# Spatial mamba: two blocks of states scanned by one instruction across two PSUM banks

## The chip, the cores and the metric

The kernel runs on one core of a Trainium2 chip. The metric is the time on the device in microseconds (us) of one execution of the whole program, which computes four layers one after the other. The change touches one stage of the last layer.

## The reference, cut to what matters

The input is 4 images of 64 channels and 128 x 128 pixels. Layer 0 is an attention with a gate in the frequency domain, layer 1 a Fourier mixer with experts, layer 2 a low-pass filter, layer 3 two mamba branches, spatial and spectral, and their merging. The spatial branch treats all 65,536 pixels as one sequence, with 128 inner channels and 16 states per channel:

```python
xz = x @ in_w.T; xi, z = split(xz, 2)
xc = silu(causal_conv4(xi) + conv_b)
dt, Bm, Cm = split(xc @ xproj_w.T, [4, 20])
dt = softplus(dt @ dt_w.T + dt_b)
A = -exp(A_log)
dA  = exp(dt[..., None] * A)                       # decay
dBx = dt[..., None] * Bm[:, :, None, :] * xc[..., None]
h = dA_t * h + dBx_t                               # for each t, in order: the scan
y = einsum('bds,bs->bd', h, C_t) + xc * D
out = (y * silu(z)) @ out_w.T
```

## The kernel before, in words

Each engine has its own instruction queue and runs in order; semaphores join them. The program is a row of stages, each ended by a barrier over all engines. The changed stage is `spatial_mamba`.

**Tiling.** A long run of equal tokens in each image row (60 of them) is folded into one column, the jump column, so that a row takes KEPT = 69 columns. A chunk is 7 rows, NA = 483 columns, and there are NC = 74 chunks. The 128 channels x 16 states are 2048 recurrences. They are laid out as NBL = 16 blocks of 128 partitions; block k holds 8 channels with 16 states each. Blocks are handled as NP = 8 pairs j = 0..7 (blocks 2j and 2j + 1). Per pair and chunk:

- TensorE, `spread_dt(j)` (L2366): two matmuls with one-hot weights copy the step sizes `du[.., 0, :]` of 8 channels onto 128 partitions, into PSUM `p_d`. In the trace one fp32 matmul is two instructions. It waits until pair j - 2 has been scanned, since there are four banks of `p_d`, one for each block modulo 4.
- ScalarE, `decay` (L2495): two exponentials, in place in `p_d`, one for each block.
- TensorE, `spread_u(j)` (L2379), the same for the inputs, into `p_u`; VectorE, `feed(j)` (L2565): `p_u` times B into `bx`, both blocks by one instruction. For pair OWN = 3 the spreading is done by a transfer (`spread_own`) and the product by GpSimd (`own_feed`, L2311).
- VectorE, `scan(j)` (L2582): one `tensor_tensor_scan` for each block, `hs = p_d * state + bx`. Its start value is the last column of the same block in `hs`, left there by the chunk before; in chunk 0 it is the constant 0.0 and 32 columns are left off.
- GpSimd, `weigh(j)` (L2302): both blocks of `hs` times C into `hc`.
- TensorE, `total(q)` (L2393), for every two pairs: the sum over states into `p_y`.

Around that, per chunk: the projections of x, z, dt, B and C through `p_x` (L2329, L2330, L2335, L2341, L2350, L2355), their reads on ScalarE (`read_x` L2447 and L2448, `read_z`, `softplus_in` and `softplus_out`, `copy_b` L2482, `copy_c`, the sigmoid's logarithm and exponential), `silu` and `step_sizes` on GpSimd, the skip term (L2386), `gate` on VectorE (L2590), `project_out` (L2399) and the store.

**Order.** Each engine's order within a chunk is written out by hand in a call of `stream`, as pairs (lag, part): in the turn of chunk i, a part works on chunk i - lag. The first 10 and the last turns are written out, the middle is a loop of four chunks per turn. VectorE's order is feed(1), scan(0), feed(2), scan(1), gate of the chunk before, scan(2), feed(4), scan(3), feed(5), scan(4), feed(6), scan(5), feed(7), scan(6), feed(0) of the next chunk, scan(7). In TensorE's order spread_dt(j) mostly stands right ahead of a spread_u, with one other product behind them.

**Semaphores of the change.** `scanned` counts blocks (16 a chunk), `decay_ready` blocks, `dt_spread` pairs, `bx_ready` the seven feeds, `weighted` pairs. `after(eng, sem, n)` is a wait that is left out where n is a constant of zero or less.

Of the kernel before, what the change touches and what calls it, by code (L numbers as in the profile page):

```python
# [2121 lines left out]
def spatial_mamba(nc, x2, w_in, w_conv, w_z, conv_b, w_xd, w_dt, dt_b, w_brep, w_crep, w_b, a_log, a_log2, skip_d, w_out, one_hot, fold, ident,  # L2122
# [11 lines left out]
    with Stage(nc, "spa") as st:  # L2134
# [35 lines left out]
        bx = st.sb("bx", [128, NBL, NA])  # L2170
        hs = st.sb("hs", [128, NBL, NA])
# [8 lines left out]
        p_d = [st.ps(f"p_d{i}", [128, 512]) for i in range(4)]  # L2180
# [10 lines left out]
        (dt_spread, u_spread, decay_ready, bx_ready, scanned, weighted, summed, y_ready, out_done, out_copied) = (  # L2191
            st.sem(n) for n in ("dt_spread", "u_spread", "decay_ready", "bx_ready", "scanned", "weighted", "summed", "y_ready",
# [15 lines left out]
        def kept(t):  # L2208
            return t.rearrange("p k (r w) -> p k r w", w=KEPT)[:, :, :, 0:KEPT - 1]

# [53 lines left out]
        def _(pool):  # L2264
# [27 lines left out]
            def weigh(j0, j1):  # L2292

                def run(c, s, r):
                    if j0 == 0:
                        pool.wait_ge(c_copied, c + 1)
                    for j in range(j0, j1):
                        pool.wait_ge(scanned, c * NBL + (2 * j + 2))

                        after(pool, summed, c * 4 + (j // 2 - 1))  # L2300
                        k = 2 * j
                        nc.gpsimd.tensor_tensor(hc[:, k % 8:k % 8 + 2, :], hs[:, k:k + 2, :],  # L2302
                                                cr2[:, s % 2, :].unsqueeze(1).broadcast_to([128, 2, NA]), ALU.mult).then_inc(weighted, 1)
                return run

            def own_feed(c, s, r):
                pool.wait_ge(b_copied, c + 1)
                pool.wait_ge(u_in, 32 * c + 32)

                after(pool, scanned, (c - 1) * NBL + (2 * OWN + 2))  # L2310
                nc.gpsimd.tensor_tensor(kept(bx[:, 2 * OWN:2 * OWN + 2, :]), b_kept(s), kept(uc[:, :, :]), ALU.mult).then_inc(bx_pool, 1)  # L2311
# [4 lines left out]
        def _(pe):  # L2316
# [4 lines left out]
            nc.tensor.matmul(p_d[1][:, 0:2], wd[:, :], c0[:, 0:2], start=True, stop=True).then_inc(setup_pe, 1)  # L2321
            nc.tensor.matmul(p_d[2][:, 0:ST], xrep[:, :], wb[:, :], start=True, stop=True).then_inc(setup_pe, 1)
# [34 lines left out]
            def spread_dt(j):  # L2357

                def run(c, s, r):
                    pe.wait_ge(dt_step, 2 * c + 2)  # L2360

                    after(pe, scanned, c * NBL + (2 * j - 2))
                    for e in range(2):
                        g = 2 * (j % 2) + e
                        v = slice(32 * g, 32 * g + 32)
                        mm = nc.tensor.matmul(p_d[(2 * j + e) % 4][:, 0:NA], hot[v, j // 2, :], du[v, s % 2, 0, :], start=True, stop=True)  # L2366
# [45 lines left out]
        def _(act):  # L2412
# [18 lines left out]
            nc.scalar.activation(c0[:, 4:5], p_d[1][:, 0:1], ACT.Relu, bias=db[:, 0:1])  # L2431
            link(nc.scalar.activation(c0[:, 5:6], p_d[1][:, 0:1], ACT.Abs, bias=db[:, 0:1]))
# [57 lines left out]
            def decay(j0, j1):  # L2490

                def run(c, s, r):
                    for k in range(2 * j0, 2 * j1):
                        act.wait_ge(dt_spread, c * NP + (k // 2 + 1))
                        nc.scalar.activation(p_d[k % 4][:, 0:NA], p_d[k % 4][:, 0:NA], ACT.Exp, scale=av2[:, k:k + 1]).then_inc(decay_ready, 1)  # L2495
                return run

            def copy_out(c, s, r):
# [4 lines left out]
                else:  # L2503
# [3 lines left out]
            stream(act, NC, UA, HEAD, 4, (2, decay(0, 1)), (1, softplus_in), (2, decay(1, 2)), (1, softplus_out), (2, decay(2, 3)), (0, read_x),  # L2507
                   (2, decay(3, 4)), (3, copy_out), (0, read_z), (2, decay(4, 5)), (0, sigmoid_ln), (2, decay(5, 6)), (1, copy_b),
# [3 lines left out]
        def _(dve):  # L2512
# [21 lines left out]
            link(nc.vector.tensor_scalar(b0[:, :], p_d[2][:, 0:ST], c0[:, 7:8], None, ALU.mult))  # L2534
# [17 lines left out]
            nc.vector.tensor_copy(bx[:, :, :].rearrange("p k (r w) -> p k r w", w=KEPT)[:, :, :, KEPT - 1],  # L2552
# [4 lines left out]
            def feed(j):  # L2557

                def run(c, s, r):
# [4 lines left out]
                    after(dve, scanned, (c - 1) * NBL + (2 * j + 2))  # L2564
                    nc.vector.tensor_tensor(kept(bx[:, 2 * j:2 * j + 2, :]), b_kept(s), kept(p_u[:, :, 0:NA]), ALU.mult).then_inc(bx_ready, 1)  # L2565
                return run

            def scan(j):

                def run(c, s, r):  # L2570
                    for k in (2 * j, 2 * j + 1):
                        dve.wait_ge(decay_ready, c * NBL + (k + 1))
                        if k % 2 == 0:
                            if j == OWN:
                                dve.wait_ge(bx_pool, c + 1)
                            else:
                                dve.wait_ge(bx_ready, c * ND + (FED.index(j) + 1))

                            after(dve, weighted, (c - 1) * NP + (j + 1))
                        start = isinstance(c, int) and c == 0  # L2580
                        v = slice(SHIFT if start else 0, NA)
                        nc.vector.tensor_tensor_scan(hs[:, k, v], p_d[k % 4][:, v], bx[:, k, v], 0.0 if start else hs[:, k, NA - 1:NA],  # L2582
                                                     ALU.mult, ALU.add).then_inc(scanned, 1)
# [821 lines left out]
```

## Time and profile before

| | us |
|---|---|
| median of 3 runs | 7533.4 |
| lowest and highest | 7525.0, 7562.55 |
| profiled execution, time | 7550.36 |
| its span in the trace | 7548.5 |
| VectorE / TensorE / ScalarE / GpSimd busy, whole span | 5590.7 / 6575.4 / 3977.8 / 3832.4 |

The profile is of one execution. A busy time is the union of an engine's instructions; a matmul's end is modelled, so a busy TensorE is not one at its peak. Consecutive instructions on VectorE overlap a little in the trace, so the time that one takes of its queue is the distance from its start to the next start, not its length. The granted clock is a share of TensorE's full 2.4 GHz; 0.5 is the lower level, 1.2 GHz.

### The profile page before, as it was taken

Reading aid. Unit: us, or ns where it says so; the run is one execution under the profiler, and the core shown is the slowest. Engines: PE = TensorE matmul, PEld = TensorE weight load, DVE = VectorE, ACT = ScalarE, POOL = GpSimd, SP = SyncE. Lnnn points to the kernel's source line nnn. Section 1 sums busy time; section 2 is a strip of 40 time slices with the busy share of each in tenths; the row PEclk is TensorE's granted clock in tenths of the full one; section 3 lists DMA queues with packets and bytes.
Section 4 is the critical chain, followed back from the end, with each engine's and each line's share of the span. In section 5 each row is a group of like instructions: output and inputs, shape, how many; then the busy total and the mean of one; then the engine's idle time right before and its main releaser. Section 6 shows DMA issues by size and latency. Waiting matters only on the chain. (4 is left out here: it accounts for less than half of the span.)

```text
span 7548.5 us, 120463 instructions
## 1 busy us (share of the span) xinstructions
PE 6575.4 (87%) x36560; PEld 3443.7 (46%) x36560; DVE 5590.7 (74%) x5630; ACT 3977.8 (53%) x6794; POOL 3832.4 (51%) x2716
## 2 busy tenths in 40 slices
PE   8968699999967379687999999999989999999970
PEld 7852233333345134574222222222257777777750
DVE  4653677777712278103999999999979999999974
ACT  4424466666612457103666666666655555555532
POOL 0100122222200300002888888888879999999960
PEclk9989799999978689757999999999989999999985
DMA  2243234334355523533222222222200000000016
GB/s 70 72 169 124 68 99 100 100 99 101 96 127 151 229 81 100 130 86 56 37 37 36 37 37 37 39 39 38 29 16 10 10 10 10 10 10 10 8 40 190
DMA packets 638233, 518.91 MB, mean 69 GB/s; under 512 B 249981, under 2 KB 569251, under 8 KB 629563
## 3 DMA queue, kind: packets, MB, share of 16 engines
q1 hardware_dynamic: 637947, 515.62, 27.9%
q8 instruction: 115, 1.88, 0.1%
q14 instruction: 171, 1.40, 0.1%
HBM read 304.91 MB, written 171.32 MB: 63 GB/s over the span
## 5 line engine op out<-in xcount | busy, mean ns | idle before, releaser
L2582 DVE TENSOR_TENSOR_SCAN spa_hs<-spa_p_d,spa_hs,spa_bx 128x483 f32<-128x483 f32 x1168 | 1370.3, 1223 | 21.1 <-ACT spa_p_d L2495 21.1
L2302 POOL TENSOR_TENSOR spa_hc<-spa_hs,spa_cr 128x966 f32<-128x966 f32 x592 | 1219.0, 2069 | 240.7 <-DVE spa_hs L2582 239.3
L2725 POOL TENSOR_TENSOR spe_hc<-spe_hs,spe_bcu 128x1024 f32<-128x1024 f32 x520 | 1219.7, 2362 | 64.5 <-DVE spe_hs L2937 63.5
L2937 DVE TENSOR_TENSOR_SCAN spe_hs<-spe_p_d,spe_bx 128x1024 f32<-128x1024 f32 x520 | 1161.4, 2275 | 35.0 <-ACT spe_p_d L2885 31.7
L2812 PEld LDWEIGHTS spe_p_y<-spe_idt,spe_hc 128*128 128x128 f32 x8320 | 965.1, 192 | 143.8 <-issue 143.8
L1065 DVE TENSOR_REDUCE attention_nm<-attention_p_s 128x2 f32<-128x640 f32 x1024 | 789.1, 812 | 260.2 <-PE attention_p_s L922 259.1
L2812 PE MATMUL spe_p_y<-spe_idt,spe_hc 128*128 128x128 f32 x8320 | 978.2, 276 | 0.0
L1023 ACT ACTIVATE attention_pr<-attention_p_t 128x512 f32<-128x512 f32 x1280 | 710.7, 599 | 420.3 <-PE attention_p_t L945 289.1
L2495 ACT ACTIVATE spa_p_d<-spa_p_d,spa_av 128x483 f32<-128x483 f32 x1184 | 703.9, 633 | 428.3 <-PE spa_p_d L2366 426.2
L2885 ACT ACTIVATE spe_p_d<-spe_p_d 128x896 f32<-128x896 f32 x520 | 445.5, 900 | 759.1 <-PE spe_p_d L2795 758.8
L2366 PE MATMUL spa_p_d<-spa_du,spa_hot 32*128 32x483 f32 x2368 | 657.0, 630 | 56.5 <-DVE spa_hs L2582 48.4
L2565 DVE TENSOR_TENSOR spa_bx<-spa_br,spa_p_u 128x952 f32<-128x952 f32 x518 | 589.8, 1139 | 54.0 <-PE spa_p_u L2379 42.4
L2379 PE MATMUL spa_p_u<-spa_du,spa_hot 32*128 32x483 f32 x2072 | 575.3, 631 | 11.5 <-DVE spa_bx L2565 11.4
L2924 DVE TENSOR_TENSOR spe_bx<-spe_bcu,spe_p_bc 128x1792 f32<-128x1792 f32 x260 | 525.6, 2022 | 50.1 <-ACT spe_bcu L2877 17.3
L922 PE MATMUL attention_p_s<-attention_ks,attention_qs 96*128 96x320 bf16 x2048 | 454.9, 304 | 54.4 <-DMA attention_qs<-scratch_qp 38.0
L1128 POOL TENSOR_TENSOR attention_on<-attention_os,attention_rc 128x512 f32<-128x512 f32 x128 | 162.5, 1269 | 645.4 <-DMA attention_rc<-scratch_den 410.3
L2366 PEld LDWEIGHTS spa_p_d<-spa_du,spa_hot 32*128 32x128 f32 x2368 | 185.1, 187 | 530.5 <-DVE spa_hs L2582 306.4
L962 PE MATMUL attention_p_o<-attention_pr,attention_vs 128*32 128x512 f32 x3072 | 410.3, 606 | 0.4 <-ACT attention_os L1037 0.4
L945 PE MATMUL attention_p_t<-attention_qs,attention_ks 99*128 99x512 bf16 x1024 | 396.1, 388 | 6.4 <-DMA attention_qs<-attention_mr 4.8
L1897 PE MATMUL experts_p_x<-experts_fs,experts_wx 128*128 128x512 f32 x768 | 332.6, 597 | 47.4 <-DVE experts_bx L1923 47.4
L2795 PE MATMUL spe_p_d<-spe_wa,spe_dt 32*128 32x512 f32 x2080 | 340.1, 640 | 3.4 <-DVE spe_hs L2937 3.3
L2393 PE MATMUL spa_p_y<-spa_hc,spa_fd 128*32 128x483 f32 x2368 | 308.8, 594 | 5.0 <-POOL spa_hc L2302 3.7
(425 smaller groups left out, 10630.8 us busy)
## 6 DMA issues: line engine op xcount, KB each, us to landing
attention_qs<-scratch_qp SPq DMA_DIRECT2D x768, 64.0 KB, 2.8
spa_uc<-spa_du SPq DMA_DIRECT2D x148, 241.5 KB
attention_rc<-scratch_den SPq DMA_DIRECT2D x128, 256.0 KB
scratch_qp<-patch_parts SPq DMA_DIRECT2D x64, 384.0 KB, 2.3
spa_xt<-scratch_x SPq DMA_DIRECT2D x148, 121.5 KB, 2.7
front_xs<-in_x_dram SPq DMA_DIRECT2D x64, 256.0 KB, 3.0
scratch_xf<-front_out SPq DMA_DIRECT2D x128, 128.0 KB, 2.5
patch_x<-scratch_xf SPq DMA_DIRECT2D x8, 2048.0 KB, 19.8
```

What stands on the lines that cost most here:

```text
L1023: nc.scalar.activation(pr[:, v, :], p_t[v % 2][:, :], ACT.Exp, scale=HD ** -0.5).then_inc(exp_done[v % 2], 1)
L1065: nc.vector.tensor_reduce(nm[:, c.u, t, 2 * s:2 * s + 2], p_s[s][:, :, 0:NK], AX.X, ALU.max, negate=True).then_inc(s_max[s], 1)
L2302: nc.gpsimd.tensor_tensor(hc[:, k % 8:k % 8 + 2, :], hs[:, k:k + 2, :], cr2[:, s % 2, :].unsqueeze(1).broadcast_to([128, 2, NA]), ALU.mult ...
L2366: mm = nc.tensor.matmul(p_d[(2 * j + e) % 4][:, 0:NA], hot[v, j // 2, :], du[v, s % 2, 0, :], start=True, stop=True)
L2379: mm = nc.tensor.matmul(p_u[:, e, 0:NA], hot[v, j // 2, :], du[v, s % 2, 1, :], start=True, stop=True)
L2495: nc.scalar.activation(p_d[k % 4][:, 0:NA], p_d[k % 4][:, 0:NA], ACT.Exp, scale=av2[:, k:k + 1]).then_inc(decay_ready, 1)
L2565: nc.vector.tensor_tensor(kept(bx[:, 2 * j:2 * j + 2, :]), b_kept(s), kept(p_u[:, :, 0:NA]), ALU.mult).then_inc(bx_ready, 1)
L2582: nc.vector.tensor_tensor_scan(hs[:, k, v], p_d[k % 4][:, v], bx[:, k, v], 0.0 if start else hs[:, k, NA - 1:NA], ALU.mult, ALU.add).then_ ...
L2725: nc.gpsimd.tensor_tensor(hc[:, k, :, d, :].rearrange("p s d t -> p d s t"), hs[:, k % 2, d, :, :], rows, ALU.mult)\
L2812: mm = nc.tensor.matmul(p_y[:, px], hc[:, k, n].rearrange("p d t -> p (d t)"), idt[:, :], start=False, stop=(k == NSUB - 1 and n == ST - 1))
L2924: nc.vector.tensor_tensor(bx[:, k % 2, d], steps(k, d), rows_for(p_bc[k % 2][:, 0:TD], d), ALU.mult).then_inc(bx_ready, 1)
L2937: nc.vector.tensor_tensor_scan(hs[:, k % 2, d].rearrange("p d s t -> p (d s t)"), p_d[h][:, :], bx[:, k % 2, d].rearrange("p d s t -> p (d ...
```

## The change

The two blocks of a pair are scanned by one instruction of 2 x 483 + 1 = 967 columns. `p_d` becomes two tensors of two banks each, one for each pair modulo 2. Block 2j lies in columns 28 to 510 of its two banks, block 2j + 1 in columns 512 to 994, and column 511 between them, the last of the first bank, is set to 0.0 once in the setup. `bx` and `hs` get a column more per block (stride 484). At the column between the blocks the scan computes 0 * state + bx, so that `bx[:, 2j, NA]` is the state with which block 2j + 1 starts. ScalarE puts it there: `carry(h)` copies the last states of four odd blocks of `hs`, 128 x 4, into the reset columns of `bx`, twice a chunk, for use in the next chunk. The first block's start value is still read from `hs`. Chunk 0 keeps its separate scans, without start values.

`scanned` now counts pairs (8 a chunk); all that waits for it still waits for the end of the same pair. The scan waits for the decays of both blocks of the pair before it starts (before, for each block's own), and for the new semaphore `carried`.

```diff
-        bx = st.sb("bx", [128, NBL, NA])
-        hs = st.sb("hs", [128, NBL, NA])
+        bx = st.sb("bx", [128, NBL, NA + 1])
+        hs = st.sb("hs", [128, NBL, NA + 1])
...
-        p_d = [st.ps(f"p_d{i}", [128, 512]) for i in range(4)]
+        p_d = [st.ps(f"p_d{i}", [128, 1024]) for i in range(2)]
...
+        def block_of(j, e):
+
+            o = 512 if e else 511 - NA
+            return p_d[j % 2][:, o:o + NA]
+
+        def joined(t, j):
+
+            return t[:, 2 * j:2 * j + 2, :].rearrange("p e n -> p (e n)")[:, 0:2 * NA + 1]
...
-                        pool.wait_ge(scanned, c * NBL + (2 * j + 2))
+                        pool.wait_ge(scanned, c * NP + (j + 1))
...
-                        nc.gpsimd.tensor_tensor(hc[:, k % 8:k % 8 + 2, :], hs[:, k:k + 2, :],
+                        nc.gpsimd.tensor_tensor(hc[:, k % 8:k % 8 + 2, :], hs[:, k:k + 2, 0:NA],
...
-                    after(pe, scanned, c * NBL + (2 * j - 2))
+                    after(pe, scanned, c * NP + (j - 1))
...
-                        nc.scalar.activation(p_d[k % 4][:, 0:NA], p_d[k % 4][:, 0:NA], ACT.Exp, scale=av2[:, k:k + 1]).then_inc(decay_ready, 1)
+                        nc.scalar.activation(block_of(k // 2, k % 2), block_of(k // 2, k % 2), ACT.Exp, scale=av2[:, k:k + 1]).then_inc(decay_ready, 1)
...
+            def carry(h):
+
+                def run(c, s, r):
+                    act.wait_ge(scanned, c * NP + 4 * (h + 1))
+                    k = 8 * h
+                    nc.scalar.activation(bx[:, k:k + 8:2, NA:NA + 1], hs[:, k + 1:k + 8:2, NA - 1:NA], ACT.Copy).then_inc(carried, 1)
+                return run
+
-            stream(act, NC, UA, HEAD, 4, (2, decay(0, 1)), (1, softplus_in), (2, decay(1, 2)), (1, softplus_out), (2, decay(2, 3)), (0, read_x),
-                   (2, decay(3, 4)), (3, copy_out), (0, read_z), (2, decay(4, 5)), (0, sigmoid_ln), (2, decay(5, 6)), (1, copy_b),
+            stream(act, NC, UA, HEAD, 4, (2, decay(0, 1)), (1, softplus_in), (2, decay(1, 2)), (3, carry(1)), (1, softplus_out), (2, decay(2, 3)), (0, read_x),
+                   (2, decay(3, 4)), (3, copy_out), (0, read_z), (2, decay(4, 5)), (0, sigmoid_ln), (2, decay(5, 6)), (2, carry(0)), (1, copy_b),
...
+            for i in range(2):
+                link(nc.vector.memset(p_d[i][:, 511:512], 0.0))
...
-                    for k in (2 * j, 2 * j + 1):
-                        dve.wait_ge(decay_ready, c * NBL + (k + 1))
...
+                    dve.wait_ge(decay_ready, c * NBL + (k + 2))
...
+                    if isinstance(c, int) and c == 0:
+                        for e in range(2):
+                            last = nc.vector.tensor_tensor_scan(hs[:, k + e, SHIFT:NA], block_of(j, e)[:, SHIFT:NA], bx[:, k + e, SHIFT:NA],
+                                                                0.0, ALU.mult, ALU.add)
+                    else:
+
+                        dve.wait_ge(carried, 2 * c + (j // 4 - 1))
+                        last = nc.vector.tensor_tensor_scan(joined(hs, j), p_d[j % 2][:, 511 - NA:512 + NA], joined(bx, j), hs[:, k, NA - 1:NA],
+                                                            ALU.mult, ALU.add)
+                    last.then_inc(scanned, 1)
```

## Rows read from the trace of the kernel before

**Rows 1.** The page's groups: line, engine, op, names, shapes, count | busy us, mean ns | idle before.
```profile
L2582 DVE TENSOR_TENSOR_SCAN spa_hs<-spa_p_d,spa_hs,spa_bx 128x483 f32<-128x483 f32 x1168 | 1370.3, 1223 | 21.1 <-ACT spa_p_d L2495 21.1
L2302 POOL TENSOR_TENSOR spa_hc<-spa_hs,spa_cr 128x966 f32<-128x966 f32 x592 | 1219.0, 2069 | 240.7 <-DVE spa_hs L2582 239.3
...
L2937 DVE TENSOR_TENSOR_SCAN spe_hs<-spe_p_d,spe_bx 128x1024 f32<-128x1024 f32 x520 | 1161.4, 2275 | 35.0 <-ACT spe_p_d L2885 31.7
```

**Rows 2.** Busy time by stretch, with instruction counts; then granted clock, DMA share, GB/s.
```profile
core 0: us, PE busy (x) PEld busy (x) DVE busy (x) ACT busy (x) POOL busy (x), PEclk, DMA share, GB/s
3560.00:5480.00 1920.00, 1852.18 (x7839) 551.69 (x7840) 1877.63 (x1745) 1256.20 (x2093) 1671.26 (x943) 0.97 0.25 36
3850.00:3900.00 50.00, 49.07 (x190) 13.91 (x188) 44.09 (x42) 30.22 (x50) 38.24 (x24) 0.86 0.25 36
```

**Rows 3.** Waits in the stage, 3560 to 5480 us: total us, times, longest.
```profile
ACT spa_p_d L2495 <- PE spa_p_d L2366: 416.2, 373, 4.6
PEld spa_p_d L2366 <- DVE spa_hs L2582: 306.4, 343, 1.4
POOL spa_hc L2302 <- DVE spa_hs L2582: 236.0, 241, 4.0
```

**Rows 4.** VectorE's timeline over a chunk: start us, length us, instructions merged.
```profile
5047.73 2.34 DVE L2582 TENSOR_TENSOR_SCAN spa_hs<-spa_p_d,spa_hs,spa_bx 128x483 f32<-128x483 f32 x2
...
5053.26 0.65 DVE L2590 TENSOR_TENSOR spa_y<-spa_p_y,spa_xz 128x483 f32<-128x483 f32 x1
...
5056.05 1.14 DVE L2565 TENSOR_TENSOR spa_bx<-spa_br,spa_p_u 128x952 f32<-128x952 f32 x1
5057.09 2.35 DVE L2582 TENSOR_TENSOR_SCAN spa_hs<-spa_p_d,spa_hs,spa_bx 128x483 f32<-128x483 f32 x2
5059.34 1.14 DVE L2565 TENSOR_TENSOR spa_bx<-spa_br,spa_p_u 128x952 f32<-128x952 f32 x1
...
5070.23 2.35 DVE L2582 TENSOR_TENSOR_SCAN spa_hs<-spa_p_d,spa_hs,spa_bx 128x483 f32<-128x483 f32 x2
...
5079.05 0.66 DVE L2590 TENSOR_TENSOR spa_y<-spa_p_y,spa_xz 128x483 f32<-128x483 f32 x1
```

**Rows 5.** VectorE's timeline in chunk 0.
```profile
3545.80 2.08 DVE L2582 TENSOR_TENSOR_SCAN spa_hs<-spa_p_d,spa_bx 128x451 f32<-128x451 f32 x2
3547.79 1.12 DVE L2565 TENSOR_TENSOR spa_bx<-spa_br,spa_p_u 128x952 f32<-128x952 f32 x1
```

**Rows 6.** VectorE's timeline in the spectral stage.
```profile
6013.91 4.46 DVE L2937 TENSOR_TENSOR_SCAN spe_hs<-spe_p_d,spe_bx 128x1024 f32<-128x1024 f32 x2
```

**Rows 7.** Timeline of all engines in the same chunk as rows 4.
```profile
5053.99 1.08 PE L2366 MATMUL spa_p_d<-spa_du,spa_hot 32*128 32x483 f32 x4
5055.29 1.19 ACT L2495 ACTIVATE spa_p_d<-spa_p_d,spa_av 128x483 f32<-128x483 f32 x2
5056.96 0.68 PE L2366 MATMUL spa_p_d<-spa_du,spa_hot 32*128 32x483 f32 x2
...
5058.25 1.08 PE L2386 MATMUL spa_p_y<-spa_xz,spa_dg 128*128 128x483 f32 x2
...
5067.19 1.19 ACT L2495 ACTIVATE spa_p_d<-spa_p_d,spa_av 128x483 f32<-128x483 f32 x2 [0.67 <-PE spa_p_d L2366]
```

**Rows 8.** Instructions on the states and their inputs: duration ns min/median/max, first and last start.
```profile
L2582 DVE TENSOR_TENSOR_SCAN spa_hs<-spa_p_d,spa_hs,spa_bx x1168: 1190/1222/1303, 3561.0 to 5486.3; 128x483 f32<-128x483 f32 x195
L2311 POOL TENSOR_TENSOR spa_bx<-spa_br,spa_uc x74: 2034/2126/2232, 3538.1 to 5464.8; 128x952 f32<-128x952 f32 x74
```

**Rows 9.** ScalarE's small operations in the setup.
```profile
3490.67 0.20 ACT L2433 ACTIVATE spa_c<-spa_c 128x1 f32<-128x1 f32 x1
...
3491.46 0.31 ACT L2436 ACTIVATE spa_a<-spa_av,spa_c 128x16 f32<-128x16 f32 x1 [0.36 <-DVE spa_c L2530]
```

**Rows 10.** VectorE's last step of the setup.
```profile
3502.49 0.27 DVE L2552 COPY spa_bx<-spa_jump 128x112 f32<-128x112 f32 x1 [4.45 <-DMA spa_jump<-scratch_steady]
```

**Rows 11.** TensorE's timeline in a stretch of low clock.
```profile
3848.59 1.98 PE L2366 MATMUL spa_p_d<-spa_du,spa_hot 32*128 32x483 f32 x4
```

More of the change, by code:

```diff
@@ L2308, in own_feed @@
                 pool.wait_ge(u_in, 32 * c + 32)
[L2310 to L2311 removed]
+                after(pool, scanned, (c - 1) * NP + (OWN + 1))
+                nc.gpsimd.tensor_tensor(kept(bx[:, 2 * OWN:2 * OWN + 2, 0:NA]), b_kept(s), kept(uc[:, :, :]), ALU.mult).then_inc(bx_pool, 1)
             stream(pool, NC, UA, HEAD, 2, (2, own_feed), (2, weigh(0, 1)), (1, step_sizes), (2, weigh(1, 6)), (0, silu), (2, weigh(6, 8)))
@@ L2320, in _ @@
             pe.wait_ge(step, 4)
-            nc.tensor.matmul(p_d[1][:, 0:2], wd[:, :], c0[:, 0:2], start=True, stop=True).then_inc(setup_pe, 1)
-            nc.tensor.matmul(p_d[2][:, 0:ST], xrep[:, :], wb[:, :], start=True, stop=True).then_inc(setup_pe, 1)
+            nc.tensor.matmul(p_d[0][:, 512:514], wd[:, :], c0[:, 0:2], start=True, stop=True).then_inc(setup_pe, 1)
+            nc.tensor.matmul(p_d[1][:, 0:ST], xrep[:, :], wb[:, :], start=True, stop=True).then_inc(setup_pe, 1)
             pe.wait_ge(w_ready, 1)
@@ L2365, in run @@
                         v = slice(32 * g, 32 * g + 32)
-                        mm = nc.tensor.matmul(p_d[(2 * j + e) % 4][:, 0:NA], hot[v, j // 2, :], du[v, s % 2, 0, :], start=True, stop=True)
+                        mm = nc.tensor.matmul(block_of(j, e), hot[v, j // 2, :], du[v, s % 2, 0, :], start=True, stop=True)
                     mm.then_inc(dt_spread, 1)
@@ L2562, in run @@
                     dve.wait_ge(u_spread, c * ND + (FED.index(j) + 1))
-                    after(dve, scanned, (c - 1) * NBL + (2 * j + 2))
-                    nc.vector.tensor_tensor(kept(bx[:, 2 * j:2 * j + 2, :]), b_kept(s), kept(p_u[:, :, 0:NA]), ALU.mult).then_inc(bx_ready, 1)
+                    after(dve, scanned, (c - 1) * NP + (j + 1))
+                    nc.vector.tensor_tensor(kept(bx[:, 2 * j:2 * j + 2, 0:NA]), b_kept(s), kept(p_u[:, :, 0:NA]), ALU.mult).then_inc(bx_ready, 1)
                 return run
@@ L2570, in run @@
                 def run(c, s, r):
-                    for k in (2 * j, 2 * j + 1):
-                        dve.wait_ge(decay_ready, c * NBL + (k + 1))
[L2573 to L2583, printed above, removed]
+                    k = 2 * j
+                    dve.wait_ge(decay_ready, c * NBL + (k + 2))
+                    if j == OWN:
+                        dve.wait_ge(bx_pool, c + 1)
+                    else:
+                        dve.wait_ge(bx_ready, c * ND + (FED.index(j) + 1))
+                    after(dve, weighted, (c - 1) * NP + (j + 1))
+                    if isinstance(c, int) and c == 0:
+                        for e in range(2):
+                            last = nc.vector.tensor_tensor_scan(hs[:, k + e, SHIFT:NA], block_of(j, e)[:, SHIFT:NA], bx[:, k + e, SHIFT:NA],
+                                                                0.0, ALU.mult, ALU.add)
+                    else:
+                        dve.wait_ge(carried, 2 * c + (j // 4 - 1))
+                        last = nc.vector.tensor_tensor_scan(joined(hs, j), p_d[j % 2][:, 511 - NA:512 + NA], joined(bx, j), hs[:, k, NA - 1:NA],
+                                                            ALU.mult, ALU.add)
+                    last.then_inc(scanned, 1)
                 return run
```

12 lines of the change are left out of this document (6 added, 6 removed).

## The prediction

> **What bounds the kernel now.** The first view to read is the page's list of groups, for the place of the changed instruction [rows 1]: the scan at L2582 is the costliest group of the kernel, 1168 instructions of 1.223 us, all in the spatial mamba, and the engine sat idle only 21.1 us before them. The second is the table by stretches [rows 2]: over 1920 us of this stage VectorE is busy 97.8%, TensorE 96.5%, GpSimd 87%, ScalarE 65%. Two engines seem full, so the third view is what each waited for [rows 3]. TensorE waits for the scans 343 times before a spreading alone, so it follows VectorE; GpSimd waits for them too, 236 us; VectorE is idle only 1920 - 1877.6 = 42 us, half of it (21.1) for decays [rows 1]. The fourth is VectorE's own timeline [rows 4]: one chunk runs from the gate at 5053.26 to the gate at 5079.05, 25.79 us, with no idle time at all. It is made of seven feeds and eight pairs of scans and one gate. From start to start a feed takes 5057.09 - 5056.05 = 1.04, a pair of scans 5059.34 - 5057.09 = 2.25, and what is left for the gate is 25.79 - 7 x 1.04 - 8 x 2.25 = 0.51. VectorE sets the pace, and what leaves its queue leaves the span: 73 such chunks (1168 / 16) give 1883 us and the idle time 42, together 1925, and the trace has the scans of chunks 1 to 73 from 3561.0 to 5486.3 + 1.2, 1926.5 us [rows 8].
>
> **What the joined scan costs.** No row shows a scan of 967 columns, so its price comes from two neighbours. In chunk 0, where the start value is a constant, a pair of 451 columns takes 3547.79 - 3545.80 = 1.99, so one is 0.995 [rows 5]. In the spectral mamba a scan of 1024 columns, read straight across two PSUM banks, starts 4.46 - 2.27 = 2.19 us before the next one [rows 1, 6]. Between them each column costs (2.19 - 0.995) / 573 = 2.085 ns, and a start costs 0.995 - 451 x 0.002085 = 0.055. By the same line 483 columns with a constant would take 1.062; the real one, whose start value is read from hs, takes 2.25 / 2 = 1.125, so reading it costs 0.063 and the whole start 0.118. The joined scan has one start and one column more: 967 x 0.002085 + 0.118 = 2.134. Against 2.25 that saves 0.116 us a pair. The upper bound of what a start can be is this same 0.118, so a pair can't save more; the lower bound of the start that goes is 0.055, if the value from hs should turn out to be paid for elsewhere; and nothing at all is the far end. I take 0.116, since the rows on either side of 967 columns give it, and the one of 1024 has the bank boundary in it. Over 8 x 73 = 584 pairs: 68 us. Chunk 0 keeps its 16 separate scans.
>
> The Trainium skill, "Vector Engine (DVE) Microarchitecture Reference", section 5.2, gives a cost of about 75 ns per instruction after overlap, whatever the program. By that rule a pair would save 0.075 less one column, 0.073, and the change 43 us instead of 68; it lies between the 0.055 and the 0.118 of the rows here.
>
> **The wait for the second decay.** Block 2j's scan used to wait for its own decay alone; now it waits for both. The place to look is where a decay is nearest to its scan. In the chunk shown, TensorE starts the spreading for pair 3 at 5053.99, ScalarE's two decays run 5055.29 to 5056.48, and the pair's scans start at 5057.09 [rows 4, 7]: 0.61 spare with both decays done. The timeline has more to spare at the other pairs (at pair 7 decays end 5068.38, scans start 5070.23: 1.85). So the new wait costs nothing as things stand. But VectorE comes earlier now. The chain to that decay starts at the end of pair 0's scan (5050.07: spreading 2, the projection of x, two reads of x on ScalarE, the decays) and takes 6.41 us, none of them VectorE's pairs; on VectorE there lie 7.02 us, with two pairs of scans in them. 7.02 - 2 x 0.116 - 6.41 = 0.38, or some 0.3 after the semaphore. The cover holds; were it gone, each tenth of a microsecond would cost 7 us over 73 chunks, and what would be late next is pair 3's release of the spreading for pair 5.
>
> **TensorE.** It is idle 1920 - 1852 = 68 us, 0.93 a chunk [rows 2], and VectorE's speed-up takes 0.93, so by the busy share alone it would be full. But it has something to give back: where a spreading for the decays and one for a feed need not wait for each other, they run together, all eight matmuls from 5056.96 to the next product at 5058.25 in 1.29 us, while one spreading alone takes 1.08 [rows 7]; wherever TensorE is late, more of them meet. From spreading 2, released by pair 0's scan, to spreading 7, released by pair 5's, VectorE gets faster by 5 x 0.116 = 0.6 us, so TensorE comes at most 0.6 late there, where 1.85 is spare. No release point moves: each is the end of the same pair.
>
> **GpSimd.** It waits 236 us for scans, 3.2 a chunk [rows 3]; the new chunk takes away 8 x 0.116 = 0.93 and leaves 2.3. Reading hs in rows of 484 with a gap of one column is priced by its other product of nearly the same size, whose output has gaps too: median 2.13, at most 2.23, against a mean of 2.07 [rows 1, 8]. That is at most 0.16 x 8 = 1.3 us a chunk, still under what is left.
>
> **The carries.** ScalarE gets two copies of 128x4 per chunk, 148 in all. Nearest rows: 0.20 for one column, 0.31 for sixteen [rows 9]; I take 0.25. Both stand behind decays whose own spreadings already waited for the scans that the carries wait for, so the wait is over when they come. Queued behind the one are the softplus and decay 2, behind the other the copy of B (for which TensorE's next product waits) and decay 6; ScalarE idles 416 us, 5.7 a chunk, for the spreadings before its decays [rows 3], and these idle times take the copies in. The scans ask for the carry half a chunk later or more. Cost nothing; without that cover, 2 x 0.25 x 73 = 36 us at worst. The two memsets of the reset column lie ahead of a 4.45 us wait for a transfer in the setup [rows 10], which covers them: nothing.
>
> **The clock.** TensorE's granted clock is 0.97 over the stage; it falls in some stretches, such as to a mean of 0.86 at 3850 to 3900, where VectorE was busy only 44.09 of 50 us [rows 2]. At the half level (1.2 GHz) TensorE is the bound: four spreading matmuls took 1.98 us there, against 1.08 [rows 7, 11]. 0.97 stands for 6% of the time at half clock, some 115 us or 4.4 chunks, in which the shorter scans bring nothing: -4 us.
>
> **Sum.** 68 - 4 = 64 us. The profiled execution took 7550.4 us (7548.5 of span), so its like would take 7486; it lies 17 us above the median shown, and the stage doesn't differ by that in kind, so I take the same 64 from the median: 7533.4 - 64 = 7469. A measurement of this kernel can tell some 0.5%, 38 us, from no change: the line is at 7496.
>
> **Rivals.** (1) Forecast: VectorE stays the bound and a pair costs 2.13: 7469, own range 7450 to 7492; chance 0.68. (2) Only the plain start goes, 0.053 us a pair: 31 us less, 7502. For it: the reading of the start value might overlap with the first of two scans and not be saved. Against it: both scans of a pair read it today and each shows 1.12. Chance 0.10. The rule of the skill cited above would give 7490. (3) A chain takes over: decays for pair 3 late, or GpSimd, or the carries; 0.4 to 0.9 us per chunk given back, 7500 to 7533. Against it the margins above (0.3 at pair 3, 2.3 less 1.3 on GpSimd, ScalarE's idle time), the smallest of them worked out from differences of tenths. Chance 0.09. (4) The change does not do what it says on VectorE: the reset column or the crossing in the middle of the stream costs what the start saved, 7533; chance 0.04. (5) Slower: the stream stalls where it passes from one bank to the next. It decides from 0.116 us per joined scan, and is measurable as slower from 0.116 + 38/584 = 0.18 on; at 0.3 it gives 7533 + 584 x 0.184 = 7641. Against it, the spectral scan passes the same kind of boundary and shows no such cost. Chance 0.05. (6) The clock stays down in more or fewer stretches: VectorE's idle time is 42 us now, of which the stretch shown alone has 6; none of it gives 7431, twice as much 7511; chance 0.04, split.
>
> Faster: nearly all of (1), a little of (2), (3) and (6), 0.73; same 0.21; slower 0.06. The range for 8 in 10 reaches from the low end of (1) over (2) into (3): 7446 to 7512.
>
> **What would show it.** Right: the joined scans, 584 of them at 2.22 to 2.24 us each, 2.13 from start to next start; a full-rate chunk of 24.86 us between gates; VectorE with no idle time before the scans outside the low-clock stretches; ScalarE with 148 new instructions of about 0.25; GpSimd's waits down by 0.9 a chunk. Wrong: joined scans over 2.3 us, or a wait for the decays or for GpSimd that recurs in every chunk, or low clock in much more than 6% of the stage.

## The result: 107 us faster, 43 more than forecast

| | before | after |
|---|---|---|
| median, us | 7542.4 (4 runs) | 7435.1 (4 runs) |
| lowest and highest | 7525.0, 7562.55 | 7430.99, 7439.47 |
| ratio of the times, 95% interval | | 0.9861, 0.9839 to 0.9883 |

The change makes the kernel 1.4% faster: 107 us, where the forecast had 64. 7435 lies below the predicted range (7446 to 7512), near the 7431 that rival (6) gave for a kernel without any idle time on VectorE. The direction was right, and so was the engine. The shorter scans bring 61 of the 107 us. Most of the rest was in none of the terms of the sum.

The page's groups of the changed kernel, in the columns of [rows 1]:

```profile
L2311 POOL TENSOR_TENSOR spa_hc<-spa_hs,spa_cr 128x966 f32<-128x966 f32 x592 | 1314.1, 2240 | 41.6 <-DVE spa_hs L2605 38.7
L2605 DVE TENSOR_TENSOR_SCAN spa_hs<-spa_p_d,spa_hs,spa_bx 128x967 f32<-128x967 f32 x584 | 1304.3, 2233 | 0.7 <-ACT spa_p_d L2504 0.7
```

The joined scan is 2.233 us long, as forecast (2.22 to 2.24). The idle time before it is 0.7 us in all, where 21.1 stood before the separate scans [rows 1]: neither the wait for both decays nor the one for `carried` costs anything. GpSimd's product went from a mean of 2.07 to 2.24 us, just above the bound of the prediction (2.23).

VectorE's timeline in the changed kernel, in the columns of [rows 4]:

```profile
5000.19 2.24 DVE L2605 TENSOR_TENSOR_SCAN spa_hs<-spa_p_d,spa_hs,spa_bx 128x967 f32<-128x967 f32 x1
5002.33 1.13 DVE L2584 TENSOR_TENSOR spa_bx<-spa_br,spa_p_u 128x952 f32<-128x952 f32 x1
5003.37 2.24 DVE L2605 TENSOR_TENSOR_SCAN spa_hs<-spa_p_d,spa_hs,spa_bx 128x967 f32<-128x967 f32 x1
5005.51 0.65 DVE L2614 TENSOR_TENSOR spa_y<-spa_p_y,spa_xz 128x483 f32<-128x483 f32 x1
```

A joined scan takes 5002.33 - 5000.19 = 2.14 us of the queue. The next gate stands at 5030.46, so a chunk takes 24.95 us against 25.79 [rows 4]: 0.84 less, 0.105 a pair. Over 73 chunks that is 61 us, where the prediction's 0.116 a pair made 68.

Now the stretches. First before, then after, in the columns of [rows 2]; the first pair is the same 1200 us in both:

```profile
3900.00:5100.00 1200.00, 1157.58 (x4878) 342.57 (x4874) 1167.52 (x1085) 786.29 (x1310) 1041.31 (x588) 0.97 0.25 37
```

```profile
3900.00:5100.00 1200.00, 1135.85 (x5194) 331.84 (x5190) 1200.00 (x771) 841.10 (x1492) 1170.16 (x626) 1.00 0.26 39
3560.00:5300.00 1740.00, 1650.35 (x7538) 482.33 (x7538) 1739.98 (x1117) 1219.24 (x2164) 1696.63 (x908) 1.00 0.26 39
```

VectorE (third value) was idle 32.5 us of 1200 before and not at all after, and the granted clock went from 0.97 to 1.00. Over the whole stage VectorE's 42 us of idle time [rows 2] are gone. 61 + 42 = 103 of the 107 us. The whole stage shows it too: the scans of chunks 1 to 73 now span 5371.9 + 2.2 - 3553.2 = 1820.9 us, against 1926.5 [rows 8]. So the question left is why the idle time and the low clock went away, since nothing in the change is about them.

**Where the idle time came from.** Its place can be read in the trace of before. VectorE's timeline:

```profile
3841.31 2.42 DVE L2582 TENSOR_TENSOR_SCAN spa_hs<-spa_p_d,spa_hs,spa_bx 128x483 f32<-128x483 f32 x2
3844.85 1.15 DVE L2565 TENSOR_TENSOR spa_bx<-spa_br,spa_p_u 128x952 f32<-128x952 f32 x1 [1.12 <-issue]
...
3854.24 1.12 DVE L2565 TENSOR_TENSOR spa_bx<-spa_br,spa_p_u 128x952 f32<-128x952 f32 x1
3858.50 2.34 DVE L2582 TENSOR_TENSOR_SCAN spa_hs<-spa_p_d,spa_hs,spa_bx 128x483 f32<-128x483 f32 x2 [3.14 <-ACT spa_p_d L2495]
3863.42 1.15 DVE L2565 TENSOR_TENSOR spa_bx<-spa_br,spa_p_u 128x952 f32<-128x952 f32 x1 [2.58 <-PE spa_p_u L2379]
```

and TensorE's in the same place:

```profile
3843.88 1.08 PE L2366 MATMUL spa_p_d<-spa_du,spa_hot 32*128 32x483 f32 x4 [0.25 <-DVE spa_hs L2582]
3846.05 1.08 PE L2379 MATMUL spa_p_u<-spa_du,spa_hot 32*128 32x483 f32 x4 [1.10 <-DVE spa_bx L2565]
3847.06 1.60 PE L2393 MATMUL spa_p_y<-spa_hc,spa_fd 128*32 128x483 f32 x8
3848.59 1.98 PE L2366 MATMUL spa_p_d<-spa_du,spa_hot 32*128 32x483 f32 x4
```

Read in order of time: VectorE stands still for 1.12 us, and the releaser is "issue": the profile shows nothing that it waits for. TensorE waits 1.10 for it. Right behind, TensorE's matmuls take 1.98 instead of 1.08: the lower of the two clocks. At that clock TensorE is too slow for VectorE, which then waits 3.14 and 2.58 us. The prediction looked at this stretch (3850 to 3900 in [rows 2]) and took the low clock for its beginning.

The place of the 1.1 us is the turn of the kernel's loop. VectorE's branch at the end of a turn, once per four chunks, stands at 3839.8, 3950.4, 4058.3 and so on, 15 times, and in 10 of the 15 cases a stall of 1.0 to 1.2 us begins 3.9 us behind it. (The view of waits marks 8 of them "issue" and puts two down to VectorE's own scan.) Against a turn of 4 x 25.79 = 103.2 us, the 7 turns with a stretch of low clock take 3.0 to 7.5 us more, and the three that have such a stall alone about 1.2. A second view speaks of the same thing, the queues of transfers in 3900 to 5100; before, and then after:

```profile
q1 hardware_dynamic: 61748, 44.09, 24.7%
q14 instruction: 56, 0.46, 0.1%
```

```profile
q1 hardware_dynamic: 65623, 46.97, 26.4%
```

Before, 56 pieces of 8 KB (0.46 MB) of instructions were fetched in this stretch; after, none. The view doesn't say for which engine; that they are VectorE's is shown by e5 and e6 below, whose edits touch VectorE's queue alone. Around one turn of before, from the trace's records:

```
branch back on VectorE          5015.9
fetches of instructions, 8 KB   5017.4  5018.6  5021.3  5024.4  5070.8
VectorE stands still ("issue")  5019.77 to 5020.88
```

In the four other turns that jump back, the pieces are fetched as well, but the first of them 0.6 to 3.2 us ahead of the branch and not behind it.

Counted in the records, a turn of VectorE's loop has 294 instructions before and 235 after: 32 scans less, and 27 fewer of the instructions that handle registers and semaphores. That gives the theory.

**Theory A (pieces).** VectorE's loop was spread over too many pieces of its instruction store, so each jump back fetched instructions anew; the stall made TensorE idle, its clock fell, and that cost 3.0 to 7.5 us in each turn where it did. The change shortened the loop until it no longer fetches. **Rival B (pace).** With the joined scan TensorE or ScalarE have a different rhythm, and the clock stays up for that reason; the fetches are a side effect. **Rival C (layout).** The rows of 484 columns, or the carries on ScalarE, do it.

### The profile page after: what moved, and what is told of

The parts are those of the page before. It is cut to its first block and busy times, and to the rows that moved or that the text cites. A ratio compares the mean times of both kernels' runs of the same rounds, so it can differ in the third digit from the quotient of the medians.

```text
span 7435.4 us, 119549 instructions
## 1 busy us (share of the span) xinstructions
PE 6438.8 (87%) x36560; PEld 3391.8 (46%) x36560; DVE 5528.0 (74%) x5048; ACT 3983.0 (54%) x6942; POOL 3926.6 (53%) x2716
## 5 line engine op out<-in xcount | busy, mean ns | idle before, releaser
L2311 POOL TENSOR_TENSOR spa_hc<-spa_hs,spa_cr 128x966 f32<-128x966 f32 x592 | 1314.1, 2240 | 41.6 <-DVE spa_hs L2605 38.7
L2605 DVE TENSOR_TENSOR_SCAN spa_hs<-spa_p_d,spa_hs,spa_bx 128x967 f32<-128x967 f32 x584 | 1304.3, 2233 | 0.7 <-ACT spa_p_d L2504 0.7
```

The lines of the kernel that those rows point to most:

```text
L2605: last = nc.vector.tensor_tensor_scan(joined(hs, j), p_d[j % 2][:, 511 - NA:512 + NA], joined(bx, j), hs[:, k, NA - 1:NA], ALU.mult, ALU.add)
```

## Experiments

Each run is compared with the kernel before on the same chip; the last column gives both times. Fetches and clock are those between 3900 and 5100; the loop is given in instructions per turn, counted in the records.

| run | ratio (95%) | us, before us | VectorE's loop | fetches | clock |
|---|---|---|---|---|---|
| e1_pad | 0.9883 (0.9856 to 0.9910) | 7412.7, 7508.4 | 263 | 0 | 1.00 |
| e2_two_scans | 0.9950 (0.9934 to 0.9966) | 7471.3, 7508.4 | 267 | 0 | 1.00 |
| e3_hole | 1.0000 (0.9979 to 1.0020) | 7509.8, 7508.4 | 237 | 0 | 0.93 |
| e4_stride | 1.0004 (0.9986 to 1.0022) | 7503.5, 7508.4 | 294 | 59 | 0.97 |
| e5_pad_more | 0.9976 (0.9959 to 0.9993) | 7485.1, 7507.7 | 295 | 58 | 0.95 |
| e6_shift | 0.9950 (0.9933 to 0.9967) | 7474.3, 7507.7 | 294, moved | 0 | 1.00 |
| e7_both | 0.9826 (0.9800 to 0.9852) | 7374.5, 7507.7 | 235 | 0 | 1.00 |
| e9_changed | 0.9869 (0.9844 to 0.9894) | 7412.8, 7507.7 | 235 | 0 | 1.00 |
| e8_half_hole | 0.9869 (0.9832 to 0.9907) | 7431.1, 7525.7 | 237 | 0 | 1.00 |
| e10_two_scans_shift | 0.9938 (0.9918 to 0.9958) | 7486.4, 7525.7 | 267, moved | 0 | 1.00 |
| e11_changed_shift | 0.9867 (0.9829 to 0.9905) | 7427.0, 7525.7 | 235, moved | 0 | 1.00 |

**e1_pad: the loop lengthened by waits that are over at once.**

```diff
+                    for _ in range(2 if j < 7 else 1):
+                        dve.wait_ge(jump_in, 64)
                     last.then_inc(scanned, 1)
```

> The changed kernel with 15 more instructions per chunk in VectorE's queue, each a wait on a semaphore that was met in the setup; the work is the same. VectorE's instructions per turn of the loop go from 235 to about 295 (294 in the kernel before). Theory (length of the loop): the stalls of 1.1 us at the loop's turn come back, with fetches of instructions at every turn (five of 8 KB each as before, none in the loop of the changed kernel), and behind them stretches at the half clock; about 40 us slower than the changed kernel, 7475. Rival (tempo: the new rhythm of VectorE and TensorE keeps the clock up, the length has no part): no stall, no low clock, 7435 to 7440, as VectorE's queue runs ahead of its engine.

Measured: 7412.7, ratio 0.9883, like the changed kernel itself (e9: 0.9869). No stall, no fetch. But the loop came out at 263 instructions only, since the 15 waits of a chunk became 7 instructions, so the padding never reached the 294 at which before stalls: the run did not put the question. e5 does.

**e2_two_scans: the changed kernel, with the joined scan taken apart again.** Everything else of the change stays: layout, carries, the wait for both decays.

```diff
-                        last = nc.vector.tensor_tensor_scan(joined(hs, j), p_d[j % 2][:, 511 - NA:512 + NA], joined(bx, j), hs[:, k, NA - 1:NA],
-                                                            ALU.mult, ALU.add)
+                        for e in range(2):
+                            last = nc.vector.tensor_tensor_scan(hs[:, k + e, 0:NA], block_of(j, e), bx[:, k + e, 0:NA], hs[:, k + e, NA - 1:NA],
+                                                                ALU.mult, ALU.add)
```

> The changed kernel with the joined scan taken apart again into two scans of 483 columns, each with its start value read from hs; layout, carries and semaphores stay as changed (one wait and one count a pair). VectorE's turn of the loop: 267 instructions. The join's own share is 584 x 0.105 = 61 us by the two timelines: 7496 if the stalls at the turn stay away, and the kernel is then 46 us faster than the one before with the same scans. If 267 is as bad as 294: 7535, as before. Rival (tempo): the rhythm of the kernel before is back, so its low clock too, without any stall at the turn: 7530 or more, with fetches absent.

Measured: 7471.3, ratio 0.9950: 37 us less than before on this chip, where 46 were expected. It has the pace of before, each of 14 turns at 103.2 us (4 x 25.79), but no stall, no fetch and no low clock. The engine rhythm of before therefore does not bring the clock down by itself, which speaks against B. Its loop has 267 instructions. Layout and carries are still in it, so C stands until e4 and e6.

**e3_hole: a pause put in where the stall had been.** The changed kernel, with a memset of unused memory on VectorE at the start of each loop turn, 15 in all.

```diff
+        junk = st.sb("junk", [128, 1024])
...
+                    if j == 1 and s == 0 and not isinstance(c, int):
+                        nc.vector.memset(junk[:, :], 0.0)
```

> The changed kernel with one idle write of 1024 columns (about 1.1 us) on VectorE at the start of each turn of the loop, 15 in all, where the kernel before had its stall. Theory (a hole of 1.1 us in VectorE's stream makes TensorE wait as long, and the clock falls behind it): TensorE idle 1.1 us at each turn, half clock some 10 us later in about half of the turns, 3 to 6 us each: 16 us for the writes themselves and 25 to 40 more, 7475 to 7490. Rival (the hole alone does not bring the clock down): 16 us, 7451, granted clock 1.00 through the loop.

Measured: 7509.8, ratio 1.0000 against 0.9869 for the changed kernel (e9). 15 instructions of 0.91 us, 14 us in all, cost 1.3% or 98 us; the expectation had 41 to 56. 14 turns take 107.0 us on average, where the changed kernel has 99.8 in every one. TensorE in this kernel:

```profile
4024.01 1.08 PE L2389 MATMUL spa_p_u<-spa_du,spa_hot 32*128 32x483 f32 x4 [0.91 <-DVE spa_bx L2587]
4025.02 1.84 PE L2403 MATMUL spa_p_y<-spa_hc,spa_fd 128*32 128x483 f32 x8
4026.79 1.98 PE L2376 MATMUL spa_p_d<-spa_du,spa_hot 32*128 32x483 f32 x4
```

and the waits in 3560 to 5300 (total, times, longest):

```profile
DVE spa_hs L2608 <- ACT spa_p_d L2505: 49.7, 20, 4.0
...
DVE spa_bx L2587 <- PE spa_p_u L2389: 40.2, 24, 2.1
```

The same picture as in before: 0.91 us without work for TensorE, then matmuls at the lower clock, then VectorE waiting up to 4.0 us for a decay and 2.1 for a spreading, 90 us in all. There is no fetch in the loop here. The clock fell in 11 of 14 turns, each time right behind TensorE's 0.91 us; the other three turns are 100.8 us long, the pause and little more. So the second half of theory A is shown by itself: a pause of about a microsecond on VectorE is paid many times over, through TensorE's clock.

**e4_stride: the kernel before, with rows of 484 columns in `hs`.**

```diff
-        hs = st.sb("hs", [128, NBL, NA])
+        hs = st.sb("hs", [128, NBL, NA + 1])
...
-                        nc.gpsimd.tensor_tensor(hc[:, k % 8:k % 8 + 2, :], hs[:, k:k + 2, :],
+                        nc.gpsimd.tensor_tensor(hc[:, k % 8:k % 8 + 2, :], hs[:, k:k + 2, 0:NA],
```

> The kernel before with rows of 484 instead of 483 columns in hs alone. GpSimd's product of hs and C went from 2.07 to 2.24 us in the changed kernel. If the place of the rows in memory does that: 2.24 here as well, and the time stays, since GpSimd has over 2 us of waits a chunk: within 0.3% of 7542. Rival (the longer scan on VectorE slows GpSimd): 2.07 here.

Measured: 7503.5, ratio 1.0004. The page's group:

```profile
L2302 POOL TENSOR_TENSOR spa_hc<-spa_hs,spa_cr 128x966 f32<-128x966 f32 x592 | 1316.0, 2235 | 141.5 <-DVE spa_hs L2582 139.5
```

The product's mean is 2.24 us by the layout alone, and the time doesn't move, since GpSimd waits 100 us less for the scans (139.5 against 239.3 [rows 1]), which is 592 x 0.17. The stalls and 59 fetches are there as before. Half of C falls with it.

**e5_pad_more: the changed kernel's loop lengthened to 295.** As e1, with four waits behind each scan and two behind the last.

> The changed kernel with 30 idle waits per chunk in VectorE's queue instead of 15. The trace of the first padding showed 263 instructions per turn, not 295 (two waits go into one instruction), and no stall; this one has about 290 to 295, as the kernel before (294). Theory (the loop no longer fits what VectorE's sequencer keeps, somewhere between 267 and 294): fetches at every turn, stalls of about 1 us at most turns, half clock behind them; 40 to 100 us slower than the changed kernel, since its tempo reacted more to such a hole. Rival (the register instructions or the separate decay wait made the stall): no stall, within 10 us of the changed kernel.

Measured: 7485.1, ratio 0.9976; on the same chip the changed kernel took 7412.8. VectorE's waits in 3560 to 5300, and the queue of instruction fetches in 3900 to 5100:

```profile
DVE spa_hs L2605 <- ACT spa_p_d L2504: 45.6, 21, 4.0
DVE spa_bx L2584 <- issue: 17.3, 10, 2.0
DVE spa_bx L2584 <- PE spa_p_u L2388: 8.4, 6, 2.1
```

```profile
q14 instruction: 58, 0.48, 0.1%
```

All of it is back: fetches, "issue" stalls up to 2.0 us, the clock at 0.95, the waits for decays. Joined scans and carries are in this kernel, so it is neither the pace nor the layout that keeps the changed kernel free of stalls. The price, 72 us, may hold some of the 30 waits per chunk themselves; e1 with half as many took no more than the changed kernel, and the one turn of e5 without a stall takes 99.95 us against 99.8, so it is little.

**e6_shift: the kernel before, with its loop moved and nothing else.** 64 counts on an idle semaphore in VectorE's setup, ahead of the stage's loop:

```diff
+        idle = st.sem("idle")
...
+            for _ in range(64):
+                dve.sem_inc(idle, 1)
```

> The kernel before with 64 idle counts on a semaphore of their own in VectorE's setup, so that its loop of 294 instructions lies 64 instructions, half a fetched piece of 8 KB, further on. If only the length counts: fetches and stalls as before, time within 0.3% of before. If the place counts too (294 instructions lie in three or in four pieces of 128 according to where they start): the fetches at each turn are gone, no stalls, clock 1.00, and the time falls by some 40 us with nothing else changed.

Measured: 7474.3, ratio 0.9950, 33 us less than before by instructions that do nothing. The loop has the same 294 instructions, 63 places further on as the records ahead of it are counted, and there is no fetch and no stall:

```profile
3900.00:5100.00 1200.00, 1163.99 (x5029) 348.54 (x5026) 1200.00 (x1118) 811.05 (x1351) 1072.09 (x606) 1.00 0.25 38
```

VectorE is busy throughout, each of 14 turns takes 103.2 us, and the clock is 1.00. This is the cleanest witness against B and C: the kernel before, with its own scans, rhythm and layout, loses its idle time when its loop lies elsewhere. It also shows that the length alone doesn't decide.

**e9_changed: the changed kernel again**, on the chip of e5 to e7.

> The changed kernel again, on the same chip as the three others, as their measure: 0.986 of the kernel before, no stalls at the turns, granted clock 1.00 in the loop.

Measured: 7412.8, ratio 0.9869. With e6 it splits the gain on one chip: before to e6 33.4 us (the loop's stalls and what follows from them), e6 to e9 61.5 us (the joined scan, 584 x 0.105 = 61.3 by the timelines). The whole is 94.9 there, and 107 on the first chip.

**e10_two_scans_shift and e11_changed_shift: length and place apart.** e2 with 70 such counts, which puts its loop of 267 at the place of the loop of before, counted modulo 128 instructions (8 KB of 64 bytes); and the changed kernel with 64.

> The taken-apart kernel (two scans a pair, 267 instructions per turn, no stall) with 70 idle counts in the setup. By the numbers of executed instructions its loop lay 58 instructions further on than that of the kernel before; now it lies 128 further on, which is the same place within a piece of 128. If only length decides: no fetches, no stalls. If the loop must lie in three pieces: with the loop of the kernel before starting at place o, that one had stalls at o (294 long) and none at o + 63, so o is above 90; 267 instructions stall only for o above 117, so either answer narrows o: no stall more likely (7471 on the chip where before takes 7508), stalls would give 7505.

> The changed kernel with its loop of 235 instructions moved by 64, as was done to the kernel before. Three pieces of 128 hold 235 instructions from any start, so by the theory of pieces nothing changes: no fetch in the loop, granted clock 1.00, ratio to before 0.987. Rival (its freedom from stalls is luck of place, too): fetches and stalls, 40 to 100 us slower.

Measured: 0.9938 and 0.9867, no fetch and no stall in either. e10 agrees with e2 (0.9950), e11 with e9 (0.9869). A loop of 267 doesn't stall at the place where 294 does, and the loop of 235 doesn't stall at either of two places. All of the loops fit one rule. Let o be the place modulo 128 at which the loop of before starts; the others' distances from it are counted in the records ahead of each loop:

```
length, place   294, o   295, o-5   294, o+63   267, o+58   267, o-1   263, o+59   235, o+3   235, o+66
stalls          yes      yes        no          no          no         no          no         no
```

The cases in the table are before (e4 agrees), e5, e6, e2, e10, e1, the changed kernel and e11. With o anywhere from 95 to 118, those that stall lie over four pieces of 128 instructions, and the others over three. That the pieces have 128 is read from the 8 KB of each fetch; the rule itself is fitted to eight cases, and o was not measured. What the runs show without it is that both the length and the place count. The Trainium skill ("Runtime: NRT & Kernel Launch", section "Instruction fetch mechanics") says that a taken branch whose target isn't in the store any more forces a fetch before execution goes on, and the 1.1 us behind the branches of before agree. It gives 256 instructions to a page and two pages to the store; the fetches here are of 128.

**e8_half_hole: a shorter pause.** e3 with 480 columns in the memset.

```diff
-                        nc.vector.memset(junk[:, :], 0.0)
+                        nc.vector.memset(junk[:, 0:480], 0.0)
```

> As the hole of 1024 columns, but of 480 (about 0.55 us), once a turn. That hole let TensorE idle 0.91 us in one place at each turn, and the granted clock fell in most turns, 100 us in all. If the half clock needs a hole of about 1 us on TensorE: it stays at 1.00 here and the time is that of the changed kernel and 15 x 0.55 = 8 us. If any hole does it, since VectorE then runs late against TensorE: 50 to 100 us more, as with the long one.

Measured: 7431.1, ratio 0.9869. The memset is 0.46 us long, and a turn takes 100.25 us against 99.78, so the pause costs its own length and nothing else, and the clock stays at 1.00. TensorE's idle stretches are no longer than about 0.7 us there, as in the changed kernel, and 0.91 in e3. The cost of a pause isn't in proportion to its length: half of it costs 0.47 us a turn, the whole of it 7.2 (107.0 - 99.8).

**e7_both: the start value off the scan too.** A reset column ahead of each of the two blocks, so that the scan starts with the constant 0.0 and reads both blocks' states from `bx`. 968 columns; the carries copy 128 x 8.

```diff
-                    nc.scalar.activation(bx[:, k:k + 8:2, NA:NA + 1], hs[:, k + 1:k + 8:2, NA - 1:NA], ACT.Copy).then_inc(carried, 1)
+                    nc.scalar.activation(bx[:, k:k + 8, 0:1], hs[:, k:k + 8, NA:NA + 1], ACT.Copy).then_inc(carried, 1)
...
-                        last = nc.vector.tensor_tensor_scan(joined(hs, j), p_d[j % 2][:, 511 - NA:512 + NA], joined(bx, j), hs[:, k, NA - 1:NA],
+                        last = nc.vector.tensor_tensor_scan(joined(hs, j), p_d[j % 2][:, 511 - NA:513 + NA], joined(bx, j), 0.0,
```

> The changed kernel with a reset column ahead of both blocks: 968 columns, start value a constant, the carries copy the last states of all blocks (128 x 8). By the rows, the start value read from hs costs 0.063 us and a column 0.002: VectorE's chunk falls from 24.95 to 24.46 and the stage by 36 us, 0.5% below the changed kernel. Against it: GpSimd is busy 24.35 us of the 24.95; if its product with rows that start one column further takes longer than 2.24, it becomes the bound and half or all of the gain is lost; if it takes less (the product took 1.98 or 2.16 us by its place in the kernel before), the whole gain comes.

Measured: 7374.5, ratio 0.9826, 38 us less than the changed kernel on the same chip: the fastest version of this study. VectorE's timeline and the page's groups:

```profile
5000.44 2.17 DVE L2606 TENSOR_TENSOR_SCAN spa_hs<-spa_p_d,spa_bx 128x968 f32<-128x968 f32 x1
5002.52 1.12 DVE L2585 TENSOR_TENSOR spa_bx<-spa_br,spa_p_u 128x952 f32<-128x952 f32 x1
```

```profile
L2311 POOL TENSOR_TENSOR spa_hc<-spa_hs,spa_cr 128x966 f32<-128x966 f32 x592 | 1214.8, 2068 | 111.9 <-DVE spa_hs L2606 111.4
L2606 DVE TENSOR_TENSOR_SCAN spa_hs<-spa_p_d,spa_bx 128x968 f32<-128x968 f32 x584 | 1263.2, 2163 | 2.8 <-ACT spa_p_d L2504 1.1
```

A scan takes 2.08 us of the queue, 0.06 less than with a start value read from `hs`, although it has a column more. That is the 0.063 that the prediction worked out for the reading, now measured by itself. 584 x 0.06 = 35 of the 38 us. The product on GpSimd is back at a mean of 2.07, and its idle time at 112 us instead of 42. The mean hides two durations: by the trace's records the product takes 2.23 to 2.25 us in even chunks and 1.90 in odd ones. The two kinds of chunk read C from different halves of `cr2`. In the kernel before it took 2.06 to 2.08 in even chunks, and 1.90 and 2.25 by turns in odd ones; in the changed kernel and in e4 it takes 2.23 to 2.26 in all.

## Why the prediction was right and where it failed

**Right: what bounds the kernel.** VectorE sets the pace before and after, and what leaves its queue leaves the span: 61.5 us between e6 and e9, and 61.3 by the timelines.

**Right, a tenth too large: the joined scan.** 0.105 us a pair instead of 0.116, 61 us instead of 68. The joined scan takes 2.14 of the queue where the line through the two neighbours gave 2.134, and e7 shows the 0.06 for the value read from `hs`. What the bank boundary in the middle of the stream costs is not shown by itself: the neighbour of 1024 columns has one too, so any such cost is already in the line. Together with it the joining still saves 0.105 a pair, and so rivals (2), (4) and (5) fall, and with them the 0.073 a pair that stood beside the rows.

**Right: the wait for the second decay and the carries.** 0.7 us of idle time before the scans in all, 148 carries of 0.21 us (0.25 forecast) that no engine is shown to wait for. Rival (3) didn't come.

**GpSimd: right that it hides, too small in size.** The mean of the product rises by 0.17 instead of at most 0.16, as e4 shows by the layout alone. The idle time before it fell to 41.6 us of 592 products, against 236 [rows 3]: 2.7 us a chunk instead of 0.9. Forecast and bound together (0.93 + 1.3 = 2.2) nearly have this; the text named only the first. TensorE's waits show what is next. The waits of the changed kernel in 3560 to 5300:

```profile
PEld spa_p_y L2402 <- POOL spa_hc L2311: 293.0, 279, 1.7
...
POOL spa_hc L2311 <- DVE spa_hs L2605: 29.9, 70, 0.5
```

GpSimd is busy 1696.63 of 1740 us, 97.5%, 24.3 us of a chunk of 24.95. That leaves 0.6 us a chunk: by this estimate, about as much more can leave VectorE's queue before GpSimd sets the pace, and what goes beyond it brings nothing. No run tries it; in e7 the product's older mean gives the room back.

**Failed: "The clock".** "It falls in some stretches", and from this the prediction took that a share of 6% at half clock would stay, a loss of 4 us, and left VectorE's 42 us of idle time where they were: in the sum they are worth nothing. Measured, the low clock and the 42 us both went. Rival (6), with the idle time gone, had a chance of 0.04 with both its directions. Sum and rival took VectorE's idle time for a state of the chip. It had a cause in the program: a stall of 1.1 us at the turn of VectorE's loop, shown by e5 (made anew in the changed kernel) and e6 (taken from the kernel before), and its effect on TensorE's clock, shown by e3. The prediction counted what the edit takes from VectorE in microseconds and not in instructions. The trace could have told it: waits of VectorE for no other engine, each 3.9 us behind the end of a loop turn (the turns are 103 to 111 us long), with instruction fetches around them. That the loop would become free of them was not to be had from the trace of before alone, since it hangs on the place as well as on the length; that the term was open, by all of the 42 us, was.

**Still open.** By how much the price of the stalls differs between chips and executions: before to e6 gives 33 us, and the idle time of the profiled execution 42. 4 of the 107 us, 107 - 61 - 42, have no row. Which of the fetches around the branch VectorE waited for wasn't tried, nor was o measured, so the rule of three pieces is a fit.

## What to carry to other kernels

Look for waits with no releaser, and for their period. If they stand at the turns of a hardware loop, count the instructions of that loop on that engine and look for instruction fetches: an edit that adds or removes instructions, even idle ones, can change that cost by more than its own time, and a comparison of two versions should have the loop moved once to tell the two apart.

A short pause on one engine has to be priced by what it does to the others. Here a memset of 0.46 us a turn cost 0.47 and one of 0.91 about 7, because TensorE ran dry for 0.91 us and came back at half clock.

When scans are joined, it can pay to put every start value into the data. One constant start instead of a value read from memory brought another 0.06 us a pair, on top of the 0.105 for joining.

## What the runs showed of the hardware

- VectorE's instructions are fetched in pieces of 8 KB. A loop of 267 or fewer ran without a fetch at each place tried; one of 294 fetched five pieces a turn at one place and none at another. A stall took 1.0 to 1.2 us in before, and up to 2.0 in e5.
- GpSimd's `tensor_tensor` of 128x966 took 1.90, 2.07 or 2.24 us, by where the rows of its operands lie. With `hs` in rows of 484 columns read from column 0 it took 2.23 to 2.26 in every chunk (e4, and the changed kernel). With rows of 483 (before) and with rows of 484 read from column 1 (e7) the mean was 2.07, and odd chunks had instructions of 1.90.
- TensorE's granted clock fell to the lower level right behind idle stretches of 0.91 us (e3) and 1.10 us (before), and not in e8 or the changed kernel, where idle stretches of 0.7 us recur and none is longer than 0.74. That draws no sharp line: in e5, one of 12 low stretches began behind an idle stretch of 0.68 us, with none over 0.70 in the 14 us ahead. And not each pause brought it down: 10 stalls in before, 7 low stretches. It stayed down for 7 to 21 us each time, 7 stretches with 89 us between 3600 and 5200 in before, and 11 with 215 us in e3.
- A scan of 967 columns with the boundary between two PSUM banks in the middle of its stream took 2.14 us of the queue, against 2.25 for two of 483. What the boundary itself costs is not isolated.
